# Sparse mixture stage: block input turned and split two blocks ahead, rows loaded in front of weights, last ranks on VectorE

## The reference

```python
def _L3_ffn_ref(x, gate_w, w1, w3, w2):
    logits = jnp.einsum('btd,de->bte', x, gate_w)
    probs = jax.nn.softmax(logits, axis=-1)
    expert_weights, expert_indices = jax.lax.top_k(probs, 2)
    expert_weights = expert_weights / expert_weights.sum(-1, keepdims=True)
    out = jnp.zeros_like(x)
    for i in range(8):
        wi = jnp.where(expert_indices == i, expert_weights, 0.0).sum(-1)
        h = silu(x @ w1[i]) * (x @ w3[i])
        out = out + (h @ w2[i]) * wi[..., None]
    return out
...
x = x + _L3_ffn_ref(_layernorm(x), ...)
```

## Time and profile before

| | us |
|---|---|
| median of 3 runs | 1616.33 |
| lowest and highest | 1611.57, 1621.27 |
| the profiled execution | 1614.35 |
| its span in the profile | 1612.6 |
| first rows of block 0 in SBUF | 1437.15 |
| first block_out | 1465.84 |
| block_out of step 43 | 1579.36 |
| results read back | 1600.88 |

### The profile page before, as it was taken

One profiled execution on the slowest core, in us unless ns is written; L12 is line 12 of the kernel. 1 busy time (PEld: TensorE's weight loads), 2 busy tenths in 40 slices (PEclk: granted clock), 3 DMA queues, 4 the chain that ended last, 5 costly groups with the idle time before them and its releaser, 6 DMA issues. The chain is left out here.

```text
span 1612.6 us, 24666 instructions
## 1 busy us (share of the span) xinstructions
PE 1405.3 (87%) x8205; PEld 1203.9 (75%) x8205; DVE 1096.3 (68%) x2253; ACT 957.3 (59%) x1895; POOL 517.6 (32%) x860
## 2 busy tenths in 40 slices
PE   5799898999999999899899996998898988727773
PEld 5699575898888888798688875887786877527773
DVE  3676689786666667776577775776776766536664
ACT  3456776565555555556777775665565665426661
POOL 5324522303112111422321112222434424355673
PEclk7899999999999999999999998899999999859997
DMA  6111141110000010121121000920000000034542
GB/s 160 54 39 40 45 160 61 40 60 1 4 37 21 20 40 7 35 69 52 40 79 66 26 1 16 190 31 1 6 10 1 14 1 6 9 119 154 158 155 88
DMA packets 57533, 85.22 MB, mean 53 GB/s; under 512 B 9400, under 2 KB 39536, under 8 KB 56127
## 3 DMA queue, kind: packets, MB, share of 16 engines
q1 hardware_dynamic: 54911, 79.40, 18.1%
q0 software_dynamic: 2496, 4.24, 0.8%
HBM read 57.90 MB, written 15.78 MB: 46 GB/s over the span
## 5 line engine op out<-in xcount | busy, mean ns | idle before, releaser
L1553 DVE TENSOR_TENSOR hhl<-psum,hhl 128x512 fp32r<-128x512 f32 x336 | 230.2, 686 | 94.6 <-ACT hhl L1074 92.8
L1760 PE MATMUL psum<-xh,wl 128*128 128x512 f32 (+1 forms) x520 | 203.9, 392 | 7.7 <-DVE logits L1285 4.2
L1761 PE MATMUL psum<-xl,wh 128*128 128x512 f32 (+1 forms) x528 | 202.6, 384 | 0.0
L1762 PE MATMUL psum<-xh,wh 128*128 128x512 f32 (+1 forms) x528 | 202.2, 383 | 0.0
L1074 ACT ACTIVATE hhl<-psum 128x512 fp32r<-128x512 f32 x336 | 199.4, 594 | 0.7 <-DVE psum L1549 0.7
L1146 ACT ACTIVATE hhl<-psum 128x512 fp32r<-128x512 f32 (+1 forms) x160 | 95.3, 596 | 136.9 <-PE psum L2157 136.5
L884 POOL TENSOR_SCALAR shared<-shared,xrd 128x589 f32<-128x589 f32 x128 | 97.7, 765 | 231.4 <-DVE xrd L1647 230.7
L1064 ACT ACTIVATE psum<-psum 128x512 f32<-128x512 f32 x208 | 121.2, 583 | 74.4 <-PE psum L1762 73.3
L1062 ACT ACTIVATE act_out<-psum 128x512 f32<-128x512 f32 x128 | 76.4, 598 | 119.7 <-PE psum L1762 119.3
L1549 DVE TENSOR_TENSOR psum<-act_out,psum 128x512 f32<-128x512 f32 x128 | 88.9, 695 | 84.2 <-PE psum L1762 75.7
L1652 DVE TENSOR_TENSOR hhl<-psum,hhl 128x512 fp32r<-128x512 f32 (+1 forms) x160 | 110.2, 689 | 52.1 <-ACT hhl L1146 51.8
(11 more groups left out here) (370 smaller groups left out, 3725.7 us busy)
## 6 DMA issues: line engine op xcount, KB each, us to landing
shared<-in_f_dram SPq DMA_DIRECT2D x16, 768.0 KB
shared<-comb_dram SPq DMA_DIRECT2D x10, 1024.0 KB
xs_dram<-wraw SPq DMA_DIRECT2D x2, 4615.0 KB
shared<-comb_dram SPq DMA_DIRECT2D x24, 256.0 KB, 5.4
wraw<-in_f_dram SPq DMA_DIRECT2D x8, 768.0 KB
xn<-in_f_dram SPq DMA_DIRECT2D x7, 768.0 KB
wraw<-in_f_dram SPq DMA_DIRECT2D x9, 512.0 KB
hhl<-qh SPq DMA_DIRECT2D x64, 64.0 KB, 2.0
```

The source lines that it names most:

```text
L1553: v.tensor_tensor(hl[k % 4], h_bank(f, k), hh[k % 4].bitcast(f32), ALU.subtract).then_inc(f.h_ready, 1)
L1760: mm(dst, ll, rh, start=start, stop=False)
L1761: mm(dst, lh, rl, start=False, stop=False)
L1762: return mm(dst, lh, rh, start=False, stop=stop)
```

## The change

Three things are edited.

- The input of a block is turned (`block_in`), split into high and low (`block_high`, `block_low`) two blocks ahead instead of one; `xbh` and `xbl` get a third buffer and `hit` a second. The wait for the rows' DMA on VectorE moves into block_low. Blocks 0 and 1 are both done in front of the loop.
- On SP, rows(s) stand in front of weights(s) in the loop, and the row numbers of blocks 0 to 2 are read in front of the wait for the scatter.
- The last batch is ranked by VectorE (`last_ranks`, six operations behind take_logits) and no longer by GpSimd.

```diff
@@ buffers
-        hit = wraw[:, 3064:3066]
+        hit = [wraw[:, 3064 + 2 * j:3066 + 2 * j] for j in range(2)]
-        xbh, xbl = [[w[:, j * BS:(j + 1) * BS] for j in range(2)] for w in (xh, xl)]
+        xbh, xbl = [[w[:, j * BS:(j + 1) * BS] for j in range(3)] for w in (xh, xl)]
@@ SP
-            def block_rows(s):
+            def first_row(s):
+                return sp.value_load(row_of[0:1, s:s + 1], min_val=0, max_val=XROWS - BS)
+
+            def block_rows(s, r):
                 if s >= 3:
                     sp.wait_ge(xb_lo, s - 2)
-                r = sp.value_load(row_of[0:1, s:s + 1], min_val=0, max_val=XROWS - BS)
...
             for s in range(3):
                 block_weights(s)
+            first = [first_row(s) for s in range(3)]
             sp.wait_ge(rows_out, 16 * 2 * NT)
             for s in range(3):
-                block_rows(s)
+                block_rows(s, first[s])
             for s in range(3, NBLK):
+                block_rows(s, first_row(s))
                 block_weights(s)
-                block_rows(s)
@@ GpSimd
             enter(7, 3, 3)
-            rank_routes(F3, 3)
@@ ScalarE
             def block_high(s):
                 act.wait_ge(xb_ps, s + 1)
-                if s >= 2:
-                    act.wait_ge(b_up, BK * (s - 1))
-                a.activation(xbh[s % 2], bank(7, BS), ACT.Copy).then_inc(xb_hi, 1)
+                if s >= 3:
+                    act.wait_ge(b_up, BK * (s - 2))
+                a.activation(xbh[s % 3], bank(7, BS), ACT.Copy).then_inc(xb_hi, 1)
...
             block_high(0)
+            block_high(1)
...
+                if k % 2 and s + 2 < NBLK:
+                    block_high(s + 2)
                 if k % 2 and s + 1 < NBLK:
-                    block_high(s + 1)
                     down_high(s + 1)
@@ VectorE
+            def last_ranks():
+                c = tiles(NB - 1)
+                d, m = pairs
+                lg = logits[:, c, :]
+                st.link(v.tensor_tensor(d, bcast(lg, NE, 2), bcast(lg, NE, 3), ALU.is_ge))
+                st.link(v.tensor_tensor(d, d, bcast(tri[:], TB, 1), ALU.mult))
+                st.link(v.tensor_tensor(m, d, d.rearrange("p t a b -> p t b a"), ALU.subtract))
+                st.link(v.tensor_reduce(rank[:, c, :], m, AX.X, ALU.add))
+                st.link(v.tensor_tensor(rank[:, c, :], rank[:, c, :], bcast(least[:], TB, 1), ALU.add))
+                v.tensor_scalar(rank[:, c, :], rank[:, c, :], 0.0, None, ALU.is_lt).then_inc(rank_ready, 1)
...
             take_logits(F3, 3, bank(7))
+            last_ranks()
             weigh_routes(F3, 3)
...
             def block_low(s):
-                v.tensor_tensor(hit, xb[s % 3][:, :, D + 1], slot_of[:, s, :], ALU.is_equal)
+                dve.wait_ge(slot_in[s % 3], 16 * (route_loads[s % 3] + s // 3 + 1))
+                v.tensor_tensor(hit[s % 2], xb[s % 3][:, :, D + 1], slot_of[:, s, :], ALU.is_equal)
                 dve.wait_ge(xb_hi, s + 1)
...
             down_low(0)
-            dve.wait_ge(slot_in[0], 16 * (route_loads[0] + 1))
             block_low(0)
+            block_low(1)
             for k in range(BK * NBLK + 7):
...
+                if k % 2 and s + 2 < NBLK:
+                    block_low(s + 2)
                 if k % 2 and s + 1 < NBLK:
-                    dve.wait_ge(slot_in[(s + 1) % 3], 16 * (route_loads[(s + 1) % 3] + (s + 1) // 3 + 1))
-                    block_low(s + 1)
                     down_low(s + 1)
@@ TensorE (block_up reads xbh[s % 3], xbl[s % 3])
             block_in(0)
+            block_in(1)
             for k in range(BK * NBLK + 6):
...
-                if k % 2 == 0 and k // 2 + 1 < NBLK:
-                    block_in(k // 2 + 1)
+                if k % 2 == 0 and k // 2 + 2 < NBLK:
+                    block_in(k // 2 + 2)
                 if k % 2 and k >= 7:
                     block_out((k - 7) // 2)
```

More of the change, by code:

```diff
@@ L1702, in block_low @@
             def block_low(s):
-                v.tensor_tensor(hit, xb[s % 3][:, :, D + 1], slot_of[:, s, :], ALU.is_equal)
+                dve.wait_ge(slot_in[s % 3], 16 * (route_loads[s % 3] + s // 3 + 1))
+                v.tensor_tensor(hit[s % 2], xb[s % 3][:, :, D + 1], slot_of[:, s, :], ALU.is_equal)
                 dve.wait_ge(xb_hi, s + 1)
-                st.link(v.tensor_tensor(xbl[s % 2], bank(7, BS), xbh[s % 2].bitcast(f32), ALU.subtract))
-                v.tensor_tensor(dest[:, s, :], hit, xb[s % 3][:, :, D], ALU.add).then_inc(xb_lo, 1)
+                st.link(v.tensor_tensor(xbl[s % 3], bank(7, BS), xbh[s % 3].bitcast(f32), ALU.subtract))
+                v.tensor_tensor(dest[:, s, :], hit[s % 2], xb[s % 3][:, :, D], ALU.add).then_inc(xb_lo, 1)
             def prod(k):
@@ L2225, in block_up @@
                     w = slice((2 * c + i) * P, (2 * c + i + 1) * P)
-                    ins = mm3(bank(k % 2)[:, i * BS:(i + 1) * BS], hi[:, w], lo[:, w], xbh[s % 2], xbl[s % 2])
+                    ins = mm3(bank(k % 2)[:, i * BS:(i + 1) * BS], hi[:, w], lo[:, w], xbh[s % 3], xbl[s % 3])
                 ins.then_inc(b_gate, 1)
@@ L2232, in block_up @@
                     ins = mm3(bank(BLOCK_BANKS[k % 3])[:, i * BS:(i + 1) * BS], hi[:, w], lo[:, w],
-                              xbh[s % 2], xbl[s % 2])
+                              xbh[s % 3], xbl[s % 3])
                 ins.then_inc(b_up, 1)
```

## The result

The changed kernel takes 1604.09 us (median of 14 runs, 1597.79 to 1609.47); the kernel before, in as many runs, 1614.86. The ratio is 0.9934, with a 95% interval of 0.992 to 0.9949: 10.8 us less by the medians. The forecast was 1604.5, from a sum of 10.8 us. Times here are medians of the fast runs; one run of part 3 alone took 2811.57 us and is left out.

A forecast was written before the change was run, and what follows sets the result against it. The sparse stage was taken as bound by a loop of waits, block_out standing behind prod, low and block_low. 3.4 + 0.55 + 5.3 + 1.55 = 10.8 us gave 1603.5 from the profiled 1614.35; forecast 1604.5, range 1597 to 1611.

The forecast's parts named there:

- The middle: Sparse stage from the first block_out on: block_out still waits for block_low, unchanged at 6.31 us a block.
- Rival (a): The middle loses block_out's stall too, all 26.4 us of it, giving 1579 us; chance 0.06.
- The start: Steps 0 to 7, up to the first block_out: up matmuls stop waiting for block_low, gain 5.3 us.
- The end: From step 43 to the last eight sends: no block_in precedes block_out, its wait goes, gain 1.55 us.
- Ranks: Last batch's routing: six VectorE operations replace nine on GpSimd, gain 3.4 us, ends 2.5 and 3.8.
- SP: Between scatter's landing and first rows' DMA: value_load moves under the wait for the scatter, gain 0.55 us.
- Rival (b): Each block: GpSimd's up_low falls onto VectorE's down_low, costing 20 us over 18 blocks, 1624 us; chance 0.06.
- Rival (c): Start gains nothing through late loads 4 to 6 or a clock drop; 0 to 2 us remain, 1607 to 1609; chance 0.16.

The follow-up runs named there:

- part 3 alone: The kernel before with only the last batch's ranks moved from GpSimd to VectorE; 1611.91 us, ratio 0.9985.
- part 1 alone: The changed kernel with the SP order and ranks of before, leaving only the block input two ahead; 1608.4 us, ratio 0.9956.
- the two pairs: block_high before gate, block_low before prod, on changed kernel and kernel before: 1599.33 and 1601.48 us; with hit and dest also behind down_low: 1581.89 and 1586.37.
- dest late alone: The changed kernel with hit and dest behind down_low, block_high and block_low in their old place; 1596.99 us, ratio 0.9882.
- block_low early: The changed kernel with block_high before gate and block_low before prod on odd steps; 1599.33 us, ratio 0.9906.
- dest late: The changed kernel with block_high before gate, block_low before prod on odd steps, and hit and dest behind down_low; 1581.89 us, ratio 0.9791.

## Why the prediction was right

**The middle.** Right, and the point that decided the case. The 0.24 us in the table lies in its first block (6.61 before, 6.30 after). The lead of two blocks changes the number in block_out's wait and not its time, since block_low(s+2) stands where block_low(s+1) stood: 6.29 us a block before and after. The experiments show it from three sides. Lead alone leaves the wait (part 1 alone). The place of block_low shortens it to 0.84 us, and with dest out of the way it is gone, with either lead (the two pairs). And shortening what stands before xb_lo by 0.31 shortens the block by 0.30 (dest late alone). Rival (a) would have needed that move, not this one.

**The start**, 4.97 for 5.3. The table load was hidden as I had it: gate(0) came 0.68 us later against the rows' landing (0.70 forecast). It starts 0.02 us after the load's end at 1432.17. The drain that the Trainium skill puts behind a load (ScalarE: Activation LUTs, What ACT_TABLE_LOAD costs) is not in this trace; here the measurement decides. Load 4 was the bound, and up_high(4) began 15.2 us after the first rows landed (forecast 15.75). ScalarE's wait was shorter, 1.33 instead of 2.3, as it got there 0.4 later and the load landed 0.5 sooner than I had it. What I left out is the 0.6 us in step 5 and 0.4 in step 7 by which GpSimd held up `hit`. These two misses have opposite signs, and that the term came out within 0.33 is in part luck, as is the sum of 10.8 against 10.77 measured; measured against the unchanged start of part 3 alone, the gain would be 4.41. The clock stayed at its upper level from 1434.3 on, with no idle time of TensorE above 1.71 us behind it.

**The end**, 1.79 in the table for 1.55. The wait of 1.34 and the moved block_in went, and the sends moved up with them.

**Ranks**, 3.14 for 3.4: 0.19 of the difference is the transposed operand, within the ends given. **SP**, 0.56 between the scatter's landing and the DMA (0.73 to 0.17), as forecast 0.55; the scatter landed 0.17 later behind its last send, which eats part of it in the table.

**Rival (b)** did not come, as down_low kept its 0.47 us of distance. But its mechanism is real, and it decided the size of the next step: where block_low came under up_low, 1.56 us per block went to `dest`.

**Rival (c)** did not come either: it needed loads 2.5 us later than I put them, and load 4 landed 0.5 us sooner.

The profiled execution's first part, 5.87 us faster in unchanged code, would have made a reader of the two spans claim 16.5 us.

## What to carry to other kernels

A buffer that two kinds of work share in turn ties them together: to prefetch one of them earlier does nothing, as long as its release still comes at the same place of the other engine's program. Ask of each wait where its releaser stands in that program, and move that; here that move, with two tiny operations put out of the way, took 31 us off the kernel before (1586.37 against 1617.31), and the deeper prefetch nothing in the middle. Count from the first instruction that the change can touch, since the execution before it may vary by more than the change gives.

## What the runs showed of the hardware

A VectorE tensor_tensor whose two inputs both lie in SBUF, once GpSimd's tensor_tensor is running, stands still until that ends, however small it is. Two columns take 1.72 us instead of 0.16, 0.78 or 0.52 instead of 0.15, and end within 0.03 us of GpSimd's. 128x512 takes 1.30 instead of 0.68, and took 2.85 before the change; both end some 0.55 us behind GpSimd's. A `hit` that began 0.10 us ahead of L901 kept its 0.14. But after the change a 128x512 that began at 1420.71, 0.33 us ahead of GpSimd's instruction and still under the last scatter send, took 3.25 us and ended 0.56 behind it as well. An operation whose other input is PSUM keeps its time under the same GpSimd instruction (0.42 for xl, 0.68 for prod and low). GpSimd's instruction itself is hardly longer (2.38 to 2.43 us).

GpSimd's indirect DMAs are held up in turn. If such an operation of VectorE has been running for 0.08 us or more when the send begins, and runs on for 0.1 or more, the send ends 0.83 to 0.89 us behind it: 1.20 us in all with block_low early, 1.26 with dest late, 1.43 and 1.46 in the cases above, against 0.97. One that begins behind the send's start doesn't lengthen it: 0.99 before the change, with a whole down_low inside. This is read from the timelines of all the kernels here; no run was made to try it alone. In dest-late it costs 0.29 us of the 5.14 a block, and no run moved down_low off the send.
